# One activation table for the whole projection, and the last row's steps of the projection placed between the first scans

## The chip, the cores and the metric

The kernel runs on one core of a Trainium2 chip. Its engines work side by side, each through its own queue in order: TensorE (PE), VectorE (DVE), ScalarE (ACT), GpSimd (POOL) and SyncE (SP), which issues DMAs. They wait for one another on semaphores. The metric is the device time of one execution in microseconds (us); lower is better.

## The reference, cut to what matters

The program is a residual chain of four layers on a (4, 1024, 128) tensor: a state-space layer (`_L0_attn_a_ref`), a mixture of experts, a long convolution, the mixture again. The change touches the first layer alone.

```python
x_in = jnp.einsum('bsd,de->bse', x, w_in)              # x is layer-normed
proj = jnp.einsum('bsd,dp->bsp', x_in, w_x)
dt_low, Bm, Cm = jnp.split(proj, [DT_RANK, DT_RANK + D_STATE], axis=-1)
dt = jax.nn.softplus(jnp.einsum('bsr,rd->bsd', dt_low, w_dt) + b_dt) * (DT_MAX - DT_MIN) + DT_MIN
A = -jnp.exp(A_log)
...
def step(h, inp):
    dtt, ut, bt, ct = inp
    dA = dtt[:, :, None] * A
    barA = jnp.exp(dA)
    inp_term = jnp.einsum('bdn,bn,bd->bn', dA, bt, ut)
    h = barA * h + inp_term[:, None, :]
    y = jnp.einsum('bdn,bn->bd', h, ct) + Dp * ut
    return (h, y)
...
x = x + _L0_attn_a_ref(_layernorm(x, axis=-1), ...)
```

## The kernel before, in words

The four batch entries are called rows 0 to 3, each of 1024 tokens. `project` prepares them one after the other, `scan` runs the recurrence; both are queued on the same engines without a barrier between them.

Row b goes through `project` in these steps. DVE normalizes it and PE transposes it, ACT copies it (`tokens`), and PE multiplies it by four folded weights, each in two halves of 512 tokens. The results land in PSUM banks 2 to 5, from which ACT takes them (`projections`: Abs L326, then three copies L328 to L332) and DVE takes the positive part of the first (`positive`, L388). The softplus is max(z,0) + ln(1 + exp(-|z|)): ACT makes the exponential over 1024 columns (`exponential`, L338) and the logarithm (`logarithm`, L306), and DVE adds (`softplus`, L395). DVE multiplies by u (`step_times_u`, L402, tile `dtu`), PE multiplies that by A (`step_products`, L491) and DVE multiplies the result into the scan's input term (`input_rows`, L412).

The step sizes are also split into three bf16 parts in one buffer, `part`: ACT casts the first (`first_part`, L311), POOL subtracts (`remainder`, L268), ACT casts the second (`second_part`, L315), DVE makes the third (`third_part`, L407). SP then stores `part` to DRAM (`steps`, L244), waits until it has landed, counts up `parts_free`, and loads it back in another layout (`stack`, three DMAs, L248). There is one `part` buffer for all rows, so `first_part` of row b waits until `parts_free` has counted b stores. After the fourth row SP issues eight DMAs of zeros into `slots` (L238).

`scan` works through 16 groups of eight channels per row. For group u: PE broadcasts the steps from `stack` into two banks (`broadcast`, two matmuls, L571), ACT makes exp(scale x + bias) in place (L633, "the decay"), DVE scans 1024 steps (L668), and the result is multiplied by `c_rows` (L648), on DVE for u = 1, 4, 7, 10 and 13 and otherwise on POOL. The multiplication of DVE for u stands behind scan u+1. PE sums the states later (L582). Three pairs of banks go round, so `broadcast` of u needs the scan of u-3. Row 0 is written out; rows 1 to 3 are a hardware loop, and PE waits for the `stack` of all of them at the end of row 0.

The order of the work is what the code writes down. What is left of the projection's last row when scans begin is held in `late`: a table by engine that says ahead of which u of row 0 a step is queued. Before the change these are, for row 3, `first_part` (ACT, ahead of u=1), `second_part` (ACT, 3), `step_products` (PE, 3), `third_part` (DVE, 3) and `input_rows` (DVE, 4).

Of the kernel before, what the change touches and what calls it, by code (L numbers as in the profile page):

```python
# [24 lines left out]
P = 128  # L25
# [58 lines left out]
class Plan:  # L84
# [11 lines left out]
    def sb(self, name, shape, dt=F32):  # L96
        return self.memory.enter_context(self.nc.sbuf_tensor(name, shape, dt))
# [78 lines left out]
def project(plan, ps, m, t):  # L176
# [33 lines left out]
    steps_out = plan.dma_sem("steps_out")  # L210
    m["stacked"] = stacked = [plan.dma_sem(f"stacked{b}") for b in range(BATCH)]
    zero_made, half_made, rstd_done, rest_done = plan.sems("gpsimd", "zero_made half_made rstd_done rest_done")
    moments_done, xn_ready, z_taken, a_made, sp_done, dtu_done, lo_done, inp_done = plan.sems(
        "vector", "moments_done xn_ready z_taken a_made sp_done dtu_done lo_done inp_done")
    fold_psum, xt_psum, z_psum, u_psum, b_psum, c_psum, q_psum = plan.sems(
        "tensor", "fold_psum xt_psum z_psum u_psum b_psum c_psum q_psum")
    fold_done, xt_ready, abs_done, u_taken, b_taken, c_taken, a_exp, ln_done, hi_done, mid_done = plan.sems(
# [38 lines left out]
    @plan.on("gpsimd")  # L256
    def _(pool):
        pool.memset(m["neg_half"][:, :], -0.5).then_inc(half_made, 1)
        pool.memset(m["ones"][:, :], 1.0)
        pool.memset(zero[:, :], 0.0).then_inc(zero_made, 1)  # L260
        need(pool, half_made, 1)

        def remainder(b):

            need(pool, hi_done, b + 1)
            need(pool, lo_done, b)
            alone(plan, pool, "gpsimd")
            pool.tensor_tensor(rest[:, :], sp_all[:, bass.ds(b * SEQ, SEQ)], part[:, 0:SEQ], ALU.subtract).then_inc(rest_done, 1)  # L268

        def deviation(b):  # L270
            for q in range(2):
                need(pool, moments_done, b * 2 + (q + 1))
                pool.tensor_tensor(rstd[:, q, :], spread[:, q, :], m["neg_half"][:, 0:HT], ALU.pow).then_inc(rstd_done, 1)

        deviation(0)
        deviation(1)
        with pool.Fori(1, BATCH - 1) as b:
            for q in range(2):
                need(pool, moments_done, b * 2 + (q + 3))
                pool.tensor_tensor(rstd[:, q, :], spread[:, q, :], m["neg_half"][:, 0:HT], ALU.pow).then_inc(rstd_done, 1)  # L280
            remainder(b - 1)
        remainder(BATCH - 2)
        remainder(BATCH - 1)

    @plan.on("scalar")
    def _(act):
# [71 lines left out]
        projections(BATCH - 1, 1)  # L358
        first_part(BATCH - 2)
        exponential(BATCH - 1)  # L360
        second_part(BATCH - 2)
        logarithm(BATCH - 1)

        late["scalar"] = {1: lambda: first_part(BATCH - 1), 3: lambda: second_part(BATCH - 1)}

    @plan.on("vector")
    def _(dve):
# [57 lines left out]
        for q in range(2):  # L425
# [10 lines left out]
        dve.tensor_scalar(a_range[:, :].rearrange("p (n j) -> p n j", j=GROUP), rep, DT_MAX - DT_MIN, None,  # L436
                          ALU.mult).then_inc(a_made, 1)
        for b in range(BATCH):
            if b > 0:
                positive(b, 1)  # L440
            if b + 2 < BATCH:
                dve.wait_ge(x_in[b + 2], 16)
                statistics_of(b + 2, 0)
                statistics_of(b + 2, 1)
            if 0 < b < BATCH - 1:
                positive(b + 1, 0)
            if b + 2 < BATCH:
                normalize(b + 2, 0)
                normalize(b + 2, 1)
            if b > 0:  # L450
                third_part(b - 1)
                input_rows(b - 1)
            softplus(b)
            step_times_u(b)
        late["vector"] = {3: lambda: third_part(BATCH - 1), 4: lambda: input_rows(BATCH - 1)}

    @plan.on("tensor")
    def _(pe):
# [46 lines left out]
            step_products(b - 1)  # L505
        for q in range(2):
            products(BATCH - 1, q)
        step_products(BATCH - 2)

        need(pe, c_taken, 2 * BATCH)  # L510
        need(pe, z_taken, 2 * BATCH)
        late["tensor"] = {3: lambda: step_products(BATCH - 1)}

# [22 lines left out]
def scan(plan, ps, m, t):  # L538
# [7 lines left out]
    ident = const[:, C_ID:C_ID + P]  # L546
    h = m["states"]
    y_t = m["scratch"][:, 0:SEQ]
    diag = plan.sb("diag", [P, P])
    warm = plan.sb("warm", [P, 1])  # L550
    dt_psum, summed, y_psum = plan.sems("tensor", "dt_psum summed y_psum")
    decay_ready, y_taken = plan.sems("scalar", "decay_ready y_taken")
    scanned, prod_dve, x_added, row_moments, diag_made = plan.sems("vector", "scanned prod_dve x_added row_moments diag_made")
    prod_pool, row_pow = plan.sems("gpsimd", "prod_pool row_pow")
    n_dve, n_pool = len(ON_DVE), GROUPS - len(ON_DVE)
    group = lambda u: QG * (u % QUARTERS) + u // QUARTERS
# [63 lines left out]
    def _(act):  # L620
# [2 lines left out]
            need(act, summed, 2 * QG * b + (2 * QG - 1 + q))  # L623
            act.copy(y_t[:, q * HALF:(q + 1) * HALF], bank(ps, 6 + q)).then_inc(y_taken, 1)


        act.activation(warm[:, :], m["bias_p"][:, 0:1], ACT.Exp)
        def row(b, behind):
            for u in range(GROUPS):
                if not behind and u in m["late"]["scalar"]:  # L630
# [19 lines left out]

    @plan.on("vector")
    def _(dve):
        dve.wait_ge(m["skip_in"], 16)
        dve.tensor_scalar(diag[:, :], ident, m["skip"][:, 0:1], None, ALU.mult).then_inc(diag_made, 1)

        def add_to_x(b, q):
            need(dve, y_psum, 2 * b + (q + 1))
            rows = x[:, bass.ds(b * BT + q * HT, HT), 0:D]
# [795 lines left out]
```

## Time and profile before

| | |
|---|---|
| three runs | 553.69, 554.33 and 557.41 us, median 554.33 |
| the profiled execution | 554.59 us, of it a span of 552.7 us |
| busy in the span | PE 303.1, DVE 351.2, ACT 225.1, POOL 302.3 us |
| granted PE clock, mean | 0.73 of full speed |

The span runs from the first instruction to the last; what lies around it is 1.9 us. Projection fills the first 72 us, the scans run until 250 us, then come mixture, convolution and mixture. Queues of different engines overlap, so busy times of engines do not add up to the span; the last instruction's chain of waits does.

### The profile page before, as it was taken

Reading aid. Unit: us, or ns where it says so; the run is one execution under the profiler, and the core shown is the slowest. Engines: PE = TensorE matmul, PEld = TensorE weight load, DVE = VectorE, ACT = ScalarE, POOL = GpSimd, SP = SyncE. Lnnn points to the kernel's source line nnn. Section 1 sums busy time; section 2 is a strip of 40 time slices with the busy share of each in tenths; the row PEclk is TensorE's granted clock in tenths of the full one; section 3 lists DMA queues with packets and bytes.
Section 4 is the critical chain, followed back from the end, with each engine's and each line's share of the span. In section 5 each row is a group of like instructions: output and inputs, shape, how many; then the busy total and the mean of one; then the engine's idle time right before and its main releaser. Section 6 shows DMA issues by size and latency. Waiting matters only on the chain.

```text
span 552.7 us, 5200 instructions
## 1 busy us (share of the span) xinstructions
PE 303.1 (55%) x1283; PEld 154.3 (28%) x1283; DVE 351.2 (64%) x793; ACT 225.1 (41%) x335; POOL 302.3 (55%) x217
## 2 busy tenths in 40 slices
PE   4888552655766656656931394007788665129500
PEld 3333110111111110115820152003466564116300
DVE  5495589999999999996540085035459865207600
ACT  2768972545344445411200393009574211029400
POOL 2141145687686686684577157735342765725772
PEclk9988865777777877876555599557888776559955
DMA  7003436500000000006512231060011202123100
GB/s 202 4 1 114 135 95 225 202 1 1 0 0 0 0 0 0 0 0 180 146 55 63 93 109 43 16 159 1 0 39 38 67 27 69 54 98 91 56 18 9
DMA packets 32148, 33.27 MB, mean 60 GB/s; under 512 B 5574, under 2 KB 25053, under 8 KB 32124
## 3 DMA queue, kind: packets, MB, share of 16 engines
q1 hardware_dynamic: 27228, 25.39, 15.5%
q0 software_dynamic: 4096, 6.90, 3.8%
q10 hardware_dynamic: 800, 0.71, 0.5%
q8 instruction: 9, 0.15, 0.1%
q14 instruction: 15, 0.12, 0.1%
HBM read 14.43 MB, written 20.19 MB: 63 GB/s over the span
## 4 chain that ended last, share of the span: by engine, by line
POOL 15%; PE 13%; issue 12%; DVE 5%; ACT 4%; DMA 3%; DVEq 1%; POOLq 0%; ACTq 0%; SPq 0%
POOL slots L899 7%; POOL out L1085 4%; POOL answers L1085 3%; PE ps L1215 2%; PE ps L1283 2%; PE ps L925 2%; PE ps L1005 2%; PE ps L989 1%; ACT scaled L1027 1%; PE ps L996 1%; PE ps L1303 1%; PE ps L810 1%; DMA slots<-x,put 1%; DVE stats L729 1%; DMA x<-answers 1%
## 5 line engine op out<-in xcount | busy, mean ns | idle before, releaser
L648 POOL TENSOR_TENSOR states<-states,c_rows 128x1024 f32<-128x1024 f32 x44 | 119.0, 2707 | 51.1 <-DVE states L668 51.1
L668 DVE TENSOR_TENSOR_SCAN states<-ps,inp 128x1024 f32<-128x1024 f32 x64 | 142.2, 2271 | 2.7 <-ACT ps L633 2.7
L633 ACT ACTIVATE ps<-ps,bias_p,scale_p 128x1024 f32<-128x1024 f32 x64 | 74.5, 1176 | 88.4 <-PE ps L571 88.3
L571 PE MATMUL ps<-stack,sel 96*128 (+1 forms) x128 | 49.4, 486 | 70.0 <-DVE states L668 63.8
L899 POOL DMA_INDIRECT slots<-x,put x64 | 62.6, 978 | 33.0 <-issue 18.3
L582 PE MATMUL ps<-states,red 128*32 128x512 f32 x256 | 45.8, 811 | 1.8 <-POOL states L648 1.8
L1085 POOL DMA_INDIRECT answers<-reply,home x32 | 31.7, 990 | 24.1 <-DVE reply L1072 15.2
L1085 POOL DMA_INDIRECT out<-reply,home x32 | 31.5, 985 | 24.2 <-DVE reply L1072 15.4
L571 PEld LDWEIGHTS ps<-stack,sel 96*128 96x128 bf16 x128 | 8.9, 104 | 123.7 <-DVE states L668 90.9
L1027 ACT ACTIVATE scaled<-rows 128x128 f32<-128x128 f32 x64 | 26.4, 485 | 31.5 <-DMA rows<-slots 31.5
L729 DVE BATCH_NORM_STATS2 stats<-x 128x6 f32<-128x128 f32 x96 | 19.6, 277 | 28.1 <-DMA x<-answers 27.7
L741 POOL TENSOR_TENSOR rstd<-spread,neg_half 128x8 f32<-128x8 f32 x12 | 19.8, 1647 | 22.1 <-DVE neg_mean L735 22.1
L989 PE MATMUL ps<-const,scaled 128*128 128x128 f32 x64 | 12.1, 319 | 35.7 <-ACT scaled L1027 21.0
L1072 DVE SCALAR_TENSOR_TENSOR reply<-ps,rows,kept 128x128 f32<-128x128 f32 x64 | 18.0, 344 | 15.6 <-PE ps L1005 14.6
L268 POOL TENSOR_TENSOR rest<-states,part 128x1024 f32<-128x1024 bf16 (+1 forms) x4 | 8.5, 2127 | 33.9 <-ACT part L311 33.9
L1197 ACT ACTIVATE c_xn<-x,shift,rstd 128x128 f32<-128x128 f32 x32 | 12.7, 483 | 34.8 <-POOL shift L749 34.8
L925 PE MATMUL ps<-const,c_xn 128*128 128x128 f32 x32 | 7.8, 390 | 34.3 <-ACT c_xn L1197 34.2
L1064 DVE TENSOR_SCALAR empty<-rows 128x4 f32<-128x4 f32 x16 | 3.0, 188 | 37.0 <-DMA rows<-slots 35.7
L810 PE MATMUL ps<-w_r,rx_t 128*128 128x8 f32 x128 | 23.8, 323 | 4.3 <-ACT rx_t L933 4.3
L810 PEld LDWEIGHTS ps<-w_r,rx_t 128*128 128x128 f32 x128 | 23.0, 278 | 5.5 <-ACT rx_t L933 5.5
L648 DVE TENSOR_TENSOR states<-states,c_rows 128x1024 f32<-128x1024 f32 x20 | 24.0, 1198 | 0.0
L1241 DVE SCALAR_TENSOR_TENSOR c_s<-c_u,c_w_tap,c_s 128x1024 f32<-128x1024 f32 x16 | 19.8, 1280 | 6.2 <-ACT c_s L1232 5.9
(162 smaller groups left out, 598.5 us busy)
## 6 DMA issues: line engine op xcount, KB each, us to landing
slots<-zero SPq DMA_DIRECT2D x8, 528.0 KB
rows<-slots SPq DMA_DIRECT2D x16, 264.0 KB, 2.9
steps<-part SPq DMA_DIRECT2D x4, 768.0 KB, 3.2
stack<-steps SPq DMA_DIRECT2D x12, 256.0 KB, 4.1
x<-in_x SPq DMA_DIRECT2D x4, 512.0 KB, 6.8
answers<-x SPq DMA_DIRECT2D x4, 512.0 KB, 6.2
x<-answers SPq DMA_DIRECT2D x4, 512.0 KB, 6.1
out<-x SPq DMA_DIRECT2D x4, 512.0 KB, 3.4
```

The source lines that it names most:

```text
L571: last = pe.matmul(bank(ps, 2 * SLOTS[u] + q), sel[0:PARTS * QUARTER, (g % QG) * P:(g % QG + 1) * P], stack[:, g // QG, bass.ds(b * SEQ + ...
L582: last = pe.matmul(ps[c * QUARTER:(c + 1) * QUARTER, (6 + q) * HALF:(7 + q) * HALF], red[:, r * QUARTER:(r + 1) * QUARTER], h[:, (QUARTERS ...
L633: act.activation(slot(u), slot(u), ACT.Exp, scale=m["scale_p"][:, group(u):group(u) + 1], bias=m["bias_p"][:, group(u):group(u) + 1]).then ...
L648: eng.tensor_tensor(h[:, u * SEQ:(u + 1) * SEQ], h[:, u * SEQ:(u + 1) * SEQ], c_rows[:, bass.ds(b * SEQ, SEQ)], ALU.mult).then_inc(done, 1)
L668: dve.tensor_tensor_scan(h[:, u * SEQ:(u + 1) * SEQ], slot(u), inp[:, bass.ds(b * SEQ, SEQ)], 0.0, ALU.mult, ALU.add).then_inc(scanned, 1)
L729: dve.bn_stats(m["stats"][:, first + i, :], m["x"][:, b * BT + first + i, 0:D])
L741: return pool.tensor_tensor(m["rstd"][:, use, tiles], m["spread"][:, use, tiles], m["neg_half"][:, 0:BT], ALU.pow)
L810: last = pe.matmul(self.ps[:, self.LOGITS * HALF + i * EXPERTS:self.LOGITS * HALF + (i + 1) * EXPERTS], self.m["rx_t"][:, n % 2, i * P:(i ...
L899: pool.indirect_dma_start(out=m["slots"][n // BATCH], out_offset=bass.IndirectOffsetOnAxis(m["put"][:, q, i:i + 1], 0), in_=m["x"][:, b * ...
L1027: last = act.activation(m["scaled"][:, e % 2, j * D:(j + 1) * D], rows[:, j, 0:D], ACT.Identity, scale=rows[:, j, FACTOR:FACTOR + 1], bias ...
L1085: pool.indirect_dma_start(out=m["answers"][layer], out_offset=bass.IndirectOffsetOnAxis(m["home"][:, e, j:j + 1], 0), in_=m["reply"][:, e, ...
L1241: last = dve.scalar_tensor_tensor(out=self.s[:, q, s, :], in0=self.u[:, q, s, j:j + SEQ], scalar=self.w_tap[:, s, j:j + 1], in1=self.s[:, ...
```

## The change: what it does

A table load for a set that holds both Exp and Ln is asked for at ACT's start, and no other load stands in the program after that: the six later ones and the one-column Exp L627, which was there to load the table early, are gone. In `late`, three steps of row 3 (`logarithm`, `softplus`, `step_times_u`) and four of row 2 (`second_part`, `step_products`, `input_rows`, `third_part`) are moved from ahead of the scans to places between them, and the steps that were late before stand later. POOL's row 0 is written out so that `remainder` of row 3 can stand ahead of its u=6. The tile `diag`, which PE waits for before its first broadcast, is made two rows earlier in DVE's queue.

```diff
+        act.preload_act_table_set("natural_log_exp_and_others")
...
-        second_part(BATCH - 2)
-        logarithm(BATCH - 1)
-
-        late["scalar"] = {1: lambda: first_part(BATCH - 1), 3: lambda: second_part(BATCH - 1)}
+
+        late["scalar"] = {1: lambda: logarithm(BATCH - 1), 2: lambda: second_part(BATCH - 2), 5: lambda: first_part(BATCH - 1),
+                          10: lambda: second_part(BATCH - 1)}
...
         for b in range(BATCH):
+            if b == BATCH - 1:
+                dve.wait_ge(m["skip_in"], 16)
+                dve.tensor_scalar(m["diag"][:, :], ident, m["skip"][:, 0:1], None, ALU.mult).then_inc(m["diag_made"], 1)
             if b > 0:
                 positive(b, 1)
...
-            if b > 0:
-                third_part(b - 1)
-                input_rows(b - 1)
-            softplus(b)
-            step_times_u(b)
-        late["vector"] = {3: lambda: third_part(BATCH - 1), 4: lambda: input_rows(BATCH - 1)}
+            if b < BATCH - 1:
+                if b > 0:
+                    third_part(b - 1)
+                    input_rows(b - 1)
+                softplus(b)
+                step_times_u(b)
+        late["vector"] = {2: lambda: input_rows(BATCH - 2), 3: lambda: softplus(BATCH - 1), 4: lambda: step_times_u(BATCH - 1),
+                          5: lambda: third_part(BATCH - 2), 8: lambda: input_rows(BATCH - 1), 12: lambda: third_part(BATCH - 1)}
...
-        step_products(BATCH - 2)
...
-        late["tensor"] = {3: lambda: step_products(BATCH - 1)}
+        late["tensor"] = {1: lambda: step_products(BATCH - 2), 6: lambda: step_products(BATCH - 1)}
...
-        remainder(BATCH - 1)
+        late["gpsimd"] = {6: lambda: remainder(BATCH - 1)}
...
-        act.activation(warm[:, :], m["bias_p"][:, 0:1], ACT.Exp)
...
-        dve.wait_ge(m["skip_in"], 16)
-        dve.tensor_scalar(diag[:, :], ident, m["skip"][:, 0:1], None, ALU.mult).then_inc(diag_made, 1)
...
-        with pool.Fori(0, BATCH) as b:
+        def row(b, behind):
             for u in range(GROUPS):
+                if not behind and u in m["late"]["gpsimd"]:
+                    m["late"]["gpsimd"][u]()
                 if u not in ON_DVE:
                     multiply(pool, prod_pool, b, u)
+
+        row(0, False)
+        with pool.Fori(1, BATCH) as b:
+            row(b, True)
```

ACT's queue from the last copy of the projection on. Before (L311 is the cast of `first_part`, L315 that of `second_part`, L338 Exp, L306 Ln, L633 a decay):

```order
L332 COPY c_rows<-ps 128x512
L311 CAST part<-states 128x1024
L338 ACT_TABLE_LOAD
L338 ACTIVATE states<-states 128x1024
L315 CAST part<-rest 128x1024
L306 ACT_TABLE_LOAD
L306 ACTIVATE states<-states 128x1024
L627 ACT_TABLE_LOAD
L627 ACTIVATE warm<-bias_p 128x1
L633 ACTIVATE ps<-ps,bias_p,scale_p 128x1024
L311 CAST part<-states 128x1024
L633 ACTIVATE ps<-ps,bias_p,scale_p 128x1024 x2
```

And with the change (the same steps have the lines L313, L317, L340, L308 and L635):

```order
L334 COPY c_rows<-ps 128x512
L313 CAST part<-states 128x1024
L340 ACTIVATE states<-states 128x1024
L635 ACTIVATE ps<-ps,bias_p,scale_p 128x1024
L308 ACTIVATE states<-states 128x1024
L635 ACTIVATE ps<-ps,bias_p,scale_p 128x1024
L317 CAST part<-rest 128x1024
L635 ACTIVATE ps<-ps,bias_p,scale_p 128x1024 x3
L313 CAST part<-states 128x1024
L635 ACTIVATE ps<-ps,bias_p,scale_p 128x1024 x5
```

The three table loads are gone, the Ln and row 2's second cast stand behind decays 0 and 1, and row 3's first cast stands behind five decays, ahead of that of u=5.

DVE's queue of the same stretch with the change (L403 `dtu`, L442 `diag`, L389 `positive`, L667 a scan, L413 `input_rows`, L650 DVE's product, L396 softplus, L408 `third_part`), each row with the semaphores it waits for:

```order
L403 SCALAR_TENSOR_TENSOR dtu<-states,u 128x1024 [waits u_taken,q_psum]
L442 TENSOR_SCALAR diag<-const,skip 128x128 [waits skip_in]
L389 TENSOR_SCALAR states<-ps,b_dt 128x512 [waits abs_done]
L667 SCALAR_TENSOR_TENSOR states<-ps,inp 128x1024 [waits summed,decay_ready] x2
L413 TENSOR_TENSOR inp<-inp,ps 128x1024 [waits q_psum]
L667 SCALAR_TENSOR_TENSOR states<-ps,inp 128x1024 [waits summed,decay_ready]
L650 TENSOR_TENSOR states<-states,c_rows 128x1024 [waits scanned]
L396 TENSOR_TENSOR states<-states 128x1024 [waits ln_done]
L667 SCALAR_TENSOR_TENSOR states<-ps,inp 128x1024 [waits summed,decay_ready]
L403 SCALAR_TENSOR_TENSOR dtu<-states,u 128x1024 [waits u_taken,q_psum]
L667 SCALAR_TENSOR_TENSOR states<-ps,inp 128x1024 [waits summed,decay_ready]
L408 TENSOR_TENSOR part<-rest,part 128x1024 [waits mid_done]
```

Before, DVE went through `third_part` and `input_rows` of row 2, `softplus` and `step_times_u` of row 3 and `diag` ahead of its first scan. Now scans begin right behind `positive`, and these steps stand between them; the row that follows the last one shown is the scan of u=5.

PE's queue with the change, from the last product of the projection on (L490), with L575 the broadcasts, L497 `step_products` and L583 the first sum:

```order
L490 MATMUL ps<-scratch,w_c 128x512
L575 MATMUL ps<-stack,sel 128x512 x2
L497 MATMUL ps<-dtu,a_range 128x512 x2
L575 MATMUL ps<-stack,sel 128x512 x10
L497 MATMUL ps<-dtu,a_range 128x512 x2
L575 MATMUL ps<-stack,sel 128x512 x12
L583 MATMUL ps<-u,diag 128x512
```

Row 2's `step_products` stood ahead of the first broadcast; now it is behind it and ahead of the broadcast of u=1. That of row 3 moved from ahead of u=3 to ahead of u=6.

## Rows read from the trace of the kernel before

**Rows 1.** Stretch 115 to 160: us; busy PE, PEld, DVE, ACT, POOL; PE clock, DMA, GB/s.

```profile
115.00:160.00 45.00, 29.49 (x122) 6.15 (x118) 45.00 (x26) 21.26 (x20) 31.88 (x12) 0.77 0.00 0
```

**Rows 2.** Timeline, first table load after the start: start us, us, engine line op [idle before].

```profile
23.97 1.28 ACT L306 ACT_TABLE_LOAD   x1
...
25.27 1.06 ACT L306 ACTIVATE states<-states 128x1024 f32<-128x1024 f32 x1
26.23 0.67 ACT L326 ACTIVATE states<-ps,b_dt 128x512 f32<-128x512 f32 x1
...
26.93 0.75 DVE L388 TENSOR_SCALAR states<-ps,b_dt 128x512 f32<-128x512 f32 x1 [6.00 <-ACT states L326]
```

**Rows 3.** Timeline of the projection's loop: PE, ACT, then DVE, each in time order.

```profile
36.31 1.98 PE L491 MATMUL ps<-dtu,a_range 128*128 128x512 f32 x4 [2.06 <-DVE dtu L402]
...
37.18 1.28 ACT L338 ACT_TABLE_LOAD   x1
...
40.98 0.59 ACT L330 COPY inp<-ps 128x512 f32 x1 [0.26 <-PE ps L484]
...
48.01 1.05 ACT L311 CAST part<-states 128x1024 bf16 x1 [0.20 <-SPq L246]
...
43.40 1.23 DVE L407 TENSOR_TENSOR part<-rest,part 128x1024 bf16<-128x1024 f32 x1 [0.45 <-ACT part L315]
44.54 1.21 DVE L412 TENSOR_TENSOR inp<-inp,ps 128x1024 f32<-128x1024 f32 x1
45.85 1.23 DVE L395 TENSOR_TENSOR states<-states 128x1024 f32<-128x1024 f32 x1
```

**Rows 4.** Timeline from the projection's end to the first scan: DVE, ACT, then PE.

```profile
61.21 1.23 DVE L402 SCALAR_TENSOR_TENSOR dtu<-states,u 128x1024 f32<-128x1024 f32 x1 [0.16 <-issue]
62.35 0.74 DVE L388 TENSOR_SCALAR states<-ps,b_dt 128x512 f32<-128x512 f32 x1
66.41 1.23 DVE L407 TENSOR_TENSOR part<-rest,part 128x1024 bf16<-128x1024 f32 x1 [3.31 <-ACT part L315]
...
71.38 0.28 DVE L654 TENSOR_SCALAR diag<-const,skip 128x128 f32<-128x128 f32 x1
74.13 6.65 DVE L668 TENSOR_TENSOR_SCAN states<-ps,inp 128x1024 f32<-128x1024 f32 x3 [2.47 <-ACT ps L633]
...
61.92 1.05 ACT L311 CAST part<-states 128x1024 bf16<-128x1024 f32 x1
...
72.92 1.18 ACT L633 ACTIVATE ps<-ps,bias_p,scale_p 128x1024 f32<-128x1024 f32 x1 [2.62 <-PE ps L571]
74.03 1.03 ACT L311 CAST part<-states 128x1024 bf16<-128x1024 f32 x1
74.96 2.28 ACT L633 ACTIVATE ps<-ps,bias_p,scale_p 128x1024 f32<-128x1024 f32 x2
...
62.49 3.28 PE L491 MATMUL ps<-dtu,a_range 128*128 128x512 f32 x4 [3.36 <-DVE dtu L402]
71.87 2.72 PE L571 MATMUL ps<-stack,sel 96*128 96x512 bf16 x6 [6.10 <-issue]
```

**Rows 5.** Timeline where a DVE product, a POOL product and the late `third_part` meet.

```profile
80.70 1.20 DVE L648 TENSOR_TENSOR states<-states,c_rows 128x1024 f32<-128x1024 f32 x1
80.96 3.13 POOL L648 TENSOR_TENSOR states<-states,c_rows 128x1024 f32<-128x1024 f32 x1 [1.27 <-DVE states L668]
81.81 3.36 DVE L407 TENSOR_TENSOR part<-rest,part 128x1024 bf16<-128x1024 f32 x1
...
85.10 2.27 DVE L668 TENSOR_TENSOR_SCAN states<-ps,inp 128x1024 f32<-128x1024 f32 x1
```

**Rows 6.** `stack` DMAs: row 3's issue, all twelve's landing; then DVE where row 1 begins.

```profile
88.47 1.25 SPq L248 DMA_DIRECT2D stack<-steps  x3
...
DMA to landing us min/median/max: 3.2/4.1/5.2
...
116.95 8.83 DVE L668 TENSOR_TENSOR_SCAN states<-ps,inp 128x1024 f32<-128x1024 f32 x4
```

More of the change, by code:

```diff
@@ L212, in project @@
     zero_made, half_made, rstd_done, rest_done = plan.sems("gpsimd", "zero_made half_made rstd_done rest_done")
-    moments_done, xn_ready, z_taken, a_made, sp_done, dtu_done, lo_done, inp_done = plan.sems(
-        "vector", "moments_done xn_ready z_taken a_made sp_done dtu_done lo_done inp_done")
+    moments_done, xn_ready, z_taken, a_made, sp_done, dtu_done, lo_done, inp_done, m["diag_made"] = plan.sems(
+        "vector", "moments_done xn_ready z_taken a_made sp_done dtu_done lo_done inp_done diag_made")
+    m["diag"] = sb("diag", [P, P])
     fold_psum, xt_psum, z_psum, u_psum, b_psum, c_psum, q_psum = plan.sems(
@@ L548, in scan @@
     y_t = m["scratch"][:, 0:SEQ]
-    diag = plan.sb("diag", [P, P])
-    warm = plan.sb("warm", [P, 1])
+    diag, diag_made = m["diag"], m["diag_made"]
     dt_psum, summed, y_psum = plan.sems("tensor", "dt_psum summed y_psum")
     decay_ready, y_taken = plan.sems("scalar", "decay_ready y_taken")
-    scanned, prod_dve, x_added, row_moments, diag_made = plan.sems("vector", "scanned prod_dve x_added row_moments diag_made")
+    scanned, prod_dve, x_added, row_moments = plan.sems("vector", "scanned prod_dve x_added row_moments")
     prod_pool, row_pow = plan.sems("gpsimd", "prod_pool row_pow")
```

## The prediction, made before the changed kernel had run

> **What bounds the kernel now.** I read the stretches by engine first. While rows 1 to 3 are scanned DVE is busy for all 45 of 45 us [rows 1]: scans run at DVE's speed, so whatever changes the time at which row 1's first scan starts moves the whole rest by as much. That time is the end of the second scan's slot in the last row of [rows 6]: u=15 of row 0 starts at 116.95, and one of the four scans there takes 8.83 / 4 = 2.2 us, so row 1 starts at 119.15. I compute only how this number moves. Nothing behind it is edited.
>
> Then the timeline around the first scan. DVE stands idle twice there, 3.31 us ahead of `third_part` at 66.41 (ACT's second cast is behind a table load and an Exp) and 2.47 us ahead of the first scan [rows 4]. The first broadcast starts at 71.87, right behind `diag` (71.38 + 0.28), which is at the end of DVE's projection queue although it needs nothing of it. These 5.8 us are what the change can fill.
>
> **Part 1, the tables.** A load lasts 1.28 us, and the Ln behind the first one starts 25.27 - 23.97 = 1.30 after it [rows 2]. ACT runs through there, its next Abs at 26.23 is what DVE waited 6.00 us for, and everything behind hangs on that: 1.3 us earlier. The next loads are covered. That at 37.18 is followed by an Exp and the projection's copies, and the copies wait for PE again at 40.98 (0.26) [rows 3], so PE paces that stretch, not ACT. The Ln of row 1 feeds the softplus at 45.85, but DVE comes to that only when `third_part` and `input_rows` are through (44.54 + 1.21 = 45.75) [rows 3]; they are released by a cast that stood behind PE's products. So 0. The same pattern stands once more with row 2. The last three (Exp and Ln of row 3, and that for the decays) stand in front of work that part 2 moves, and are counted there. Part 1: **-1.3 us**.
> By the Trainium skill (ScalarE: Activation LUTs, What ACT_TABLE_LOAD costs) a switch costs a further drain, about 2.66 us in all. The trace does not agree: 1.30 from the load's start to the Ln's, with an Exp just ahead of the load. By the page's figure part 1 would be -2.7.
>
> **Part 2, the start.** `dtu` of row 2 starts at 61.21 [rows 4], now at 59.9. Behind it stand `diag` and `positive`: dtu takes 62.35 - 61.21 = 1.14 of the queue, diag about 0.2, positive 0.74. PE's first broadcast needs positive, diag and the copies that ended earlier; it starts at 59.9 + 1.14 + 0.2 + 0.74 + 0.1 = **62.1** instead of 71.87. Behind a broadcast its decay starts after 1.05 and the scan 1.21 later (71.87, 72.92, 74.13 [rows 4]), so the first scan is at 64.4 instead of 74.13: **-9.8 us**, part 1 included. ACT has its cast at 60.6 (61.92 less 1.3; it waits for `part` there) and the Exp at 61.6, done by 62.7 and in time for the decay at 63.15.
>
> **Part 3, what stands between the scans now.** Beside `third_part` and `input_rows` of row 3, which stood there before, DVE has four more steps: `input_rows` of row 2 at 1.1; `softplus` of row 3; `dtu` at 1.14 + 0.16 for the drain ahead of it [rows 4] = 1.3; `third_part` of row 2 at 1.15. The softplus stands where the late `third_part` stood before, right behind DVE's first product. There POOL, which had waited since 80.96 while the product ran to 81.9, went first, and DVE's instruction took 3.36 instead of 1.23 [rows 3, 5]; the next scan started 85.10 - 81.81 = 3.3 after it. I charge the softplus 3.3. Row 3's `third_part` is now behind the product for u=10 with POOL's for u=11 pending, the same pattern, and keeps its 3.3. Sum: 1.1 + 3.3 + 1.3 + 1.15 = **+6.9** (4.8 if the softplus, two f32 inputs from SBUF, is not held up).
>
> **Part 4, the second scan.** PE goes through `step_products` of row 2 between the first two broadcasts. The four passes took 1.98 us at 36.31 and 3.28 at 62.49, after 3.36 us of idleness [rows 3, 4]; now PE stands idle from 57.8 (62.49 - 3.36 - 1.3) to 62.1, so 3.3. A broadcast pair takes 2.72 / 3 = 0.9. The broadcast of u=1 starts at 62.1 + 0.9 + 3.3 = 66.3, its decay at 67.35, the scan at 68.6; DVE is free at 64.4 + 2.2 = 66.6. Ends: 0.7 at the fast price, 2.0 at the slow one. I take **+2.0**. ACT's Ln fits ahead of that decay.
>
> **Part 5, the sixth scan.** This decides. ACT's queue has `first_part` of row 3 ahead of the decay of u=5. That cast overwrites `part`, so it waits until row 2's store has landed; the store waits for row 2's `third_part`; and this now stands on DVE directly ahead of the scan of u=5, which needs that decay. So the round trip is open. From the start of a `third_part` to the cast released by it: 43.40 to 48.01 = 4.6 [rows 3]. Cast to decay: 74.96 - 74.03 = 0.93; decay to scan 1.21 [rows 4]. Together 6.75, less DVE's own 1.15: **+5.6**. Behind DVE's wait stands everything. Before, row 2's `third_part` ended at 67.64 and row 3's cast started at 74.03 [rows 4]: the store was long done. Lower bound 5.4: all three are measured and in a chain.
>
> **Part 6, the row boundary.** Row 3's `third_part` now stands ahead of u=12. From its end to the `stack` issue 88.47 - (81.81 + 3.36) = 3.3; the last of the three goes 0.85 later and lands after 3.2 to 5.2 [rows 6]; then 0.1 + 1.05 + 1.21 to the scan: 9.7 to 11.7 us, median 10.6. DVE has four scans and one product until then, 4 x 2.2 + 1.1 = 9.9. Before, 13 scans covered this. Ends: 0 and 1.8. The eight transfers of zeros are queued right behind this `stack` and behind no other, so I take the long side, **+1.4**.
>
> **Sum.** -9.8 + 6.9 + 2.0 + 5.6 + 1.4 = +6.1 us. The profiled execution took 554.59 us; 560.7. The median of the runs is 554.33, 0.3 lower, within what this sum can tell. A change under 1% (5.5 us, so 548.8 to 559.9) is what a measurement here can't well tell from none. As a check, DVE's idle time: 5.8 are gone and 1.3 won in front; new are 2.4 ahead of the first scan, 2.0, 5.6, 1.4 and 2.1 inside the softplus, together 13.5; 13.5 - 7.1 = 6.4.
>
> **Rivals.**
> A, as summed. 0.43.
> B, POOL gets in ahead of `dtu` too. The drain puts dtu 0.16 behind the scan's end [rows 4]; POOL's product for u=3 starts 0.18 behind such an end (80.96 against 74.13 + 6.65 = 80.78). If POOL is first, dtu takes 3.36 instead of 1.23: +2.1, **562.8**. For it: a near tie. Against: DVE leads by 0.02, and nothing here shows a SCALAR_TENSOR_TENSOR held up. 0.24.
> The Trainium skill (SBUF — State Buffer, Who interferes with whom) says that a DVE instruction with two SBUF inputs is blocked for all of a POOL instruction that reads SBUF, whoever issues first going first; by that rule B is possible, and [rows 5] agree with it in either order.
> C, the covers hold better: `stack` lands at the short end, and PE has its clock back in part 4. 6.1 - 1.4 - 1.3 = +3.4, **558.0**, within 1%. 0.16. Against it: PE's clock was down at 62.49 after less idleness.
> D, not slower, one mechanism: ACT is what paces the projection's loop, and each load ahead of row 2's dtu counts. The four I set at 0 (two Exp, two Ln) would give 4 x 1.28 = 5.1: +1.0, **555.6**. It decides once the loads hold up PE's products or DVE's softplus by over 1.3 us in all. Against it: the waits of 0.26 and 0.45 behind the loads [rows 3]. 0.09.
> E, the drain of part 1 counts: a switch gives 2.7 instead of 1.3, so +4.7, **559.3**. For it speaks no row. 0.03. That is the page's rule named in part 1.
> That the loads stay is excluded by the queue as shown. Without the round trip of part 5, and with C as well, it would be 554.6 + 3.4 - 5.6 = 552.4; I see no way to this with one `part` buffer. 0.05 for all that I have not seen, most of it on the fast side.
>
> **Numbers.** 560.7. A spreads from 559.4 to 562; of it 0.37 lies above 559.9, and all of B: slower by over 1% 0.61. C, D, E and the rest of A: within 1% 0.35. Faster 0.04. The range takes in B and its spread above and C below, 557.6 to 564.0; D and the unseen are left out.
>
> **What would show it.** First scan near 64.4. The first broadcast at 62.1 with four passes of step_products behind it. The second scan 4.2 behind the first. A wait of DVE for the decay of about 5.6 ahead of u=5, and on ACT a wait for SP ahead of its second cast in row 0. A softplus of 3.3 us, and `dtu` of 1.2 (B: 3.3). A short wait at the first scan of row 1, which starts near 125.3. ACT with one table load. I am wrong if DVE is busy through u=5, or if the first scan comes well before 64.

## The result: slower by 1.3%, near the forecast

| | us |
|---|---|
| before | 553.69 to 557.41, median 554.15 (4 runs) |
| changed | 560.45 to 564.03, median 562.44 (4 runs) |
| changed to before | 1.0129, 95% interval 1.0099 to 1.0159 |
| profiled execution of the changed kernel | 564.03, span 562.1 |

The forecast was 560.7, in a range of 557.6 to 564.0. The time went where it said: the first scan starts earlier, and DVE then waits between the scans. Two of its terms were off. The gain of 1.3 us that it took from the tables (part 1) was gone before the first scan, and the wait at the row boundary (part 6) was a microsecond longer.

DVE's timeline in the changed kernel, from the last `dtu` ahead of the scans to row 1, stands against [rows 4], [rows 5] and [rows 6]. The line numbers have shifted: L403 is `dtu`, L667 a scan, L413 `input_rows`, L650 DVE's product, L396 softplus, L408 `third_part`.

```profile
61.64 1.23 DVE L403 SCALAR_TENSOR_TENSOR dtu<-states,u 128x1024 f32<-128x1024 f32 x1 [0.16 <-issue]
62.79 0.28 DVE L442 TENSOR_SCALAR diag<-const,skip 128x128 f32<-128x128 f32 x1
62.98 0.75 DVE L389 TENSOR_SCALAR states<-ps,b_dt 128x512 f32<-128x512 f32 x1
66.09 2.29 DVE L667 TENSOR_TENSOR_SCAN states<-ps,inp 128x1024 f32<-128x1024 f32 x1 [2.36 <-ACT ps L635]
70.36 2.29 DVE L667 TENSOR_TENSOR_SCAN states<-ps,inp 128x1024 f32<-128x1024 f32 x1 [1.98 <-ACT ps L635]
72.57 1.20 DVE L413 TENSOR_TENSOR inp<-inp,ps 128x1024 f32<-128x1024 f32 x1
73.68 2.28 DVE L667 TENSOR_TENSOR_SCAN states<-ps,inp 128x1024 f32<-128x1024 f32 x1
75.88 1.20 DVE L650 TENSOR_TENSOR states<-states,c_rows 128x1024 f32<-128x1024 f32 x1
77.17 3.19 DVE L396 TENSOR_TENSOR states<-states 128x1024 f32<-128x1024 f32 x1
80.28 2.28 DVE L667 TENSOR_TENSOR_SCAN states<-ps,inp 128x1024 f32<-128x1024 f32 x1
82.72 1.23 DVE L403 SCALAR_TENSOR_TENSOR dtu<-states,u 128x1024 f32<-128x1024 f32 x1 [0.16 <-issue]
83.86 2.28 DVE L667 TENSOR_TENSOR_SCAN states<-ps,inp 128x1024 f32<-128x1024 f32 x1
86.06 1.20 DVE L408 TENSOR_TENSOR part<-rest,part 128x1024 bf16<-128x1024 f32 x1
92.75 2.29 DVE L667 TENSOR_TENSOR_SCAN states<-ps,inp 128x1024 f32<-128x1024 f32 x1 [5.48 <-ACT ps L635]
...
112.56 3.37 DVE L408 TENSOR_TENSOR part<-rest,part 128x1024 bf16<-128x1024 f32 x1
...
123.52 2.28 DVE L667 TENSOR_TENSOR_SCAN states<-ps,inp 128x1024 f32<-128x1024 f32 x1
127.67 2.29 DVE L667 TENSOR_TENSOR_SCAN states<-ps,inp 128x1024 f32<-128x1024 f32 x1 [1.87 <-ACT ps L635]
130.27 4.47 DVE L667 TENSOR_TENSOR_SCAN states<-ps,inp 128x1024 f32<-128x1024 f32 x2 [0.31 <-ACT ps L635]
```

Three bracketed waits are new (1.98, 5.48, and 1.87 with 0.31 at the row's start). Without a wait, the step behind a scan starts 2.2 us after the scan did; from 86.06 to 92.75 DVE did one step of 1.1 us.

What held up the scan of u=5 is told by the other queues: ACT's, then SP's, in the same kernel.

```profile
71.19 3.37 ACT L635 ACTIVATE ps<-ps,bias_p,scale_p 128x1024 f32<-128x1024 f32 x3
90.59 1.04 ACT L313 CAST part<-states 128x1024 bf16<-128x1024 f32 x1 [16.03 <-SPq L247]
91.54 3.36 ACT L635 ACTIVATE ps<-ps,bias_p,scale_p 128x1024 f32<-128x1024 f32 x3
...
87.29 0.34 SPq L245 DMA_DIRECT2D steps<-part  x1
90.56 1.25 SPq L249 DMA_DIRECT2D stack<-steps  x3
```

ACT sat idle for 16.03 us with the decays of u=2 to 4 done, until SP counted up `parts_free`; SP had issued the store at 87.29, when `third_part` (86.06 + 1.20) was through. ACT's idleness itself costs nothing; what costs is the decay of u=5 queued behind this cast, with DVE waiting for it.

### The profile page after: what moved, and what is told of

Same layout as the page of the kernel before. It is cut to its first block, busy times and chain, and to the rows that moved or that the text cites. A ratio compares the mean times of both kernels' runs of the same rounds, so it can differ in the third digit from the quotient of the medians.

```text
span 562.1 us, 5177 instructions
## 1 busy us (share of the span) xinstructions
PE 309.3 (55%) x1283; PEld 156.6 (28%) x1283; DVE 353.5 (63%) x793; ACT 214.4 (38%) x326; POOL 303.1 (54%) x217
## 4 chain that ended last, share of the span: by engine, by line
POOL 16%; issue 12%; PE 11%; DVE 5%; ACT 4%; DMA 3%; DVEq 1%; POOLq 0%; ACTq 0%; SPq 0%
POOL slots L904 7%; POOL out L1090 4%; POOL answers L1090 3%; PE ps L1288 2%; PE ps L1308 2%; PE ps L1001 2%; PE ps L1010 2%; DVE stats L734 1%; PE ps L815 1%; ACT scaled L1032 1%; PE ps L994 1%; PE ps L930 1%; POOL x L1266 1%; POOL c_v L1258 1%; DMA slots<-x,put 1%
## 5 line engine op out<-in xcount | busy, mean ns | idle before, releaser
L650 POOL TENSOR_TENSOR states<-states,c_rows 128x1024 f32<-128x1024 f32 x44 | 120.1, 2730 | 68.2 <-DVE states L667 68.2
L667 DVE TENSOR_TENSOR_SCAN states<-ps,inp 128x1024 f32<-128x1024 f32 x64 | 142.9, 2278 | 12.0 <-ACT ps L635 12.0
L635 ACT ACTIVATE ps<-ps,bias_p,scale_p 128x1024 f32<-128x1024 f32 x64 | 74.3, 1176 | 85.7 <-PE ps L575 85.4
L575 PE MATMUL ps<-stack,sel 96*128 (+1 forms) x128 | 50.7, 500 | 70.6 <-DVE states L667 64.4
L586 PE MATMUL ps<-states,red 128*32 128x512 f32 x256 | 48.0, 847 | 0.9 <-POOL states L650 0.9
L575 PEld LDWEIGHTS ps<-stack,sel 96*128 96x128 bf16 x128 | 9.5, 106 | 124.6 <-DVE states L667 91.6
L650 DVE TENSOR_TENSOR states<-states,c_rows 128x1024 f32<-128x1024 f32 x20 | 24.1, 1204 | 0.0
L1258 POOL TENSOR_TENSOR c_v<-c_s 128x1024 f32<-128x1024 f32 x4 | 9.4, 2354 | 25.4 <-DVE c_s L1246 25.4
```

The lines of the kernel that those rows point to most:

```text
L575: last = pe.matmul(bank(ps, 2 * SLOTS[u] + q), sel[0:PARTS * QUARTER, (g % QG) * P:(g % QG + 1) * P], stack[:, g // QG, bass.ds(b * SEQ + ...
L586: last = pe.matmul(ps[c * QUARTER:(c + 1) * QUARTER, (6 + q) * HALF:(7 + q) * HALF], red[:, r * QUARTER:(r + 1) * QUARTER], h[:, (QUARTERS ...
L635: act.activation(slot(u), slot(u), ACT.Exp, scale=m["scale_p"][:, group(u):group(u) + 1], bias=m["bias_p"][:, group(u):group(u) + 1]).then ...
L650: eng.tensor_tensor(h[:, u * SEQ:(u + 1) * SEQ], h[:, u * SEQ:(u + 1) * SEQ], c_rows[:, bass.ds(b * SEQ, SEQ)], ALU.mult).then_inc(done, 1)
L667: dve.tensor_tensor_scan(h[:, u * SEQ:(u + 1) * SEQ], slot(u), inp[:, bass.ds(b * SEQ, SEQ)], 0.0, ALU.mult, ALU.add).then_inc(scanned, 1)
```

## The experiments

Ratios are to runs of the kernel before on the same chip, with their 95% intervals. Experiments 1, 4, 5 and 9 ran on a chip on which the kernel before took 569.35 us, 2, 6, 7 and 8 on one where it took 554.78, and 3 and 10 to 12 on one where it took 554.60. So ratios, and the times of the scans in the trace, are compared, not the totals; the microseconds in the expectations are meant at the level of 554.

**1. One table alone.** To the kernel before:

```diff
+        act.preload_act_table_set("natural_log_exp_and_others")
...
-        act.activation(warm[:, :], m["bias_p"][:, 0:1], ACT.Exp)
```

> The kernel before with part 1 of the change alone: one table load, no warming Exp. Theory (PE's clock takes the gain back): DVE's positive part of row 1 starts at 25.7 instead of 26.9 and row 0's step_products at 35.05 instead of 36.31, but the four passes take 3.0 instead of 2.0 us because the granted clock is down, dtu of row 2 starts near 61.6 as in the changed kernel (61.2 before), the first scan at 74.1 to 74.6: ratio to before 1.000 to 1.001. Rival (the loss of 1.7 us between 35 and 40 us in the changed kernel is from its other edits or chance): dtu at 59.9, first scan at 72.8, ratio 0.998.

Ratio 0.9985 (0.9945 to 1.0025), which tells nothing by itself. The trace does: DVE's positive part of row 1 at 25.89, `dtu` of row 2 at 61.86, 35.97 us later, against 61.21 - 26.93 = 34.28 before [rows 2, 4]; first scan at 74.78, 0.2 us later than forecast, as is the positive part. The theory held: the gain of part 1 is made and lost again. What follows is PE's timeline in the changed kernel, where the same happens (61.64 - 25.67 = 35.97), and its stretches by engine.

```profile
31.10 0.65 PE L482 MATMUL ps<-const,scratch 128*128 128x128 f32 x4 [0.86 <-DVE scratch L382]
32.34 0.65 PE L482 MATMUL ps<-const,scratch 128*128 128x128 f32 x4 [0.59 <-DVE scratch L382]
35.05 2.97 PE L497 MATMUL ps<-dtu,a_range 128*128 128x512 f32 x4 [2.06 <-DVE dtu L403]
37.81 1.78 PE L490 MATMUL ps<-scratch,w_z 128*128 128x512 f32 x2
...
30.00:36.00 6.00, 2.49 (x11) 1.32 (x11) 5.61 (x14) 2.76 (x6) 1.89 (x2) 0.99 0.01 1
36.00:48.00 12.00, 10.47 (x27) 4.76 (x25) 9.21 (x29) 7.46 (x11) 3.32 (x3) 0.86 0.16 66
```

`step_products` of row 0 starts 1.26 us earlier than at 36.31 [rows 3], so part 1's gain had come as far as this. It then takes 2.97 instead of 1.98, and the next product 1.78 instead of 1.02. The granted clock over 36 to 48 us is 0.86 (column behind the five busy times), where the kernel before has this:

```profile
28.00:30.00 2.00, 2.00 (x4) 0.81 (x4) 1.85 (x12) 1.03 (x2) 0.22 (x1) 0.73 0.00 0
30.00:32.00 2.00, 2.00 (x3) 0.68 (x2) 1.85 (x12) 0.59 (x1) 1.54 (x2) 0.50 0.00 0
...
36.00:48.00 12.00, 9.72 (x28) 4.65 (x28) 10.92 (x33) 11.03 (x16) 4.18 (x3) 1.00 0.16 66
```

Its clock had been down too, but from 28 to 32, under products on which DVE did not wait, and was up again for `step_products`.

**2. One table, and PE given work in its pause.** To the kernel of experiment 1, in the projection's loop only (the products go to a bank that `step_products` overwrites):

```diff
+            need(pe, inp_done, b)
+            if not isinstance(b, int):
+                for twice in range(2):
+                    pe.matmul(bank(ps, 6), ident, const[:, 0:HALF], start=True, stop=True)
             need(pe, dtu_done, b + 1)
-            need(pe, inp_done, b)
...
+        pe.wait_ge(consts_in, 16)
```

> The kernel with one table alone, and two idle-time f32 matmuls (four passes, constants into the bank that step_products overwrites) in each turn of PE's projection loop, ahead of its wait for dtu. Only there: some 1.7 us of PE work in a gap of 2 to 2.6 us. In all five kernels with one table, DVE takes 36.0 us (35.7 once) from row 1's positive part to row 2's dtu, against 34.3 before. Theory (the clock is down because PE had paused between 30.2 and 35 us): it stays up, step_products take 2.0 instead of 3.0 and 3.3, and the stretch is 34.3 or less (33 if the second drop of the clock, at 49, goes as well): first scan 1.7 to 3 us earlier than in the kernel with one table. Rival (the clock falls for another reason, or the added work delays step_products): 36 us or more.

Ratio 0.993 (0.9905 to 0.9955). PE's timeline, with L492 the added products and L495 `step_products`, and the stretch behind:

```profile
33.17 1.88 PE L492 MATMUL ps<-const 128*128 128x512 f32 x4
35.32 1.99 PE L495 MATMUL ps<-dtu,a_range 128*128 128x512 f32 x4 [0.27 <-DVE dtu L403]
...
47.52 1.98 PE L495 MATMUL ps<-dtu,a_range 128*128 128x512 f32 x4 [0.72 <-DVE dtu L403]
...
36.00:48.00 12.00, 11.28 (x33) 5.19 (x32) 10.89 (x32) 8.62 (x14) 3.79 (x3) 1.00 0.16 66
```

The clock stays at full over 36 to 48 and `step_products` takes 1.99 and 1.98. From row 1's positive part (26.02) to row 2's `dtu` (58.45) it is 32.43 us, 3.54 less than with one table alone; first scan at 71.37. So the clock took back the gain of part 1. A second drop, which the kernel before has as well (3.03 for the four passes of `step_products` at 48.59), is gone too.

**3. The clock's part in the changed kernel.** The same added lines in the changed kernel.

> The changed kernel with the idle-time matmuls of the projection loop, and nothing else. Theory (the clock's part of the loss is independent of what stands between the scans): row 1's positive part to row 2's dtu in 32.4 instead of 36.0 us, the waits ahead of the second scan, of u=5 and at row 1 stay (2, 5.5, 2.3); 3.5 us less than changed: ratio to before 1.0129 - 0.0064 = 1.0065. Rival (PE's pauses are only moved, the clock is down at the first scans instead): ratio over 1.010.

Ratio 1.0068 (1.0048 to 1.0088). It is 32.44 us from the positive part to `dtu` (26.08, 58.52) instead of 35.97, and the first scan is at 62.96. The 5.48 ahead of u=5 stays, and so do the waits at row 1 (1.74 and 0.31), so what the clock costs in the projection and what the open round trip costs are two things. The wait ahead of the second scan did not stay as expected: 0.99 instead of 1.98, with `step_products` of row 2 at 3.05 instead of 3.62. That is not known to be the added products' doing. The same wait is 1.98 in the profiled executions of experiments 4 and 8 and 1.04 and 0.82 in those of 5 and 6, where nothing was edited that runs ahead of it but the name of a buffer. A single profiled execution of these kernels is uncertain by about 1 us for that reason.

**4. The cast queued later.**

```diff
-        late["gpsimd"] = {6: lambda: remainder(BATCH - 1)}
+        late["gpsimd"] = {8: lambda: remainder(BATCH - 1)}
...
-        late["scalar"] = {1: lambda: logarithm(BATCH - 1), 2: lambda: second_part(BATCH - 2), 5: lambda: first_part(BATCH - 1),
+        late["scalar"] = {1: lambda: logarithm(BATCH - 1), 2: lambda: second_part(BATCH - 2), 7: lambda: first_part(BATCH - 1),
```

> The changed kernel with row 3's first cast ahead of the decay of u=7 instead of u=5 and POOL's remainder ahead of u=8 instead of 6. Theory (the open round trip costs 5.5): the cast still waits until about 90.6 but DVE scans u=5 and 6 meanwhile; DVE's wait of 5.48 ahead of u=5 goes, at most 0.3 comes back ahead of u=7; 562.4 - 5.3 = 557.1. Rival (the wait only moves, to u=7 or to the row boundary, where the stack then lands later): 560 or more.

Ratio 1.0034 (1.0001 to 1.0068), 0.95% or 5.3 us below the changed kernel's. On DVE:

```profile
84.93 1.20 DVE L408 TENSOR_TENSOR part<-rest,part 128x1024 bf16<-128x1024 f32 x1
86.05 2.28 DVE L667 TENSOR_TENSOR_SCAN states<-ps,inp 128x1024 f32<-128x1024 f32 x1
...
89.36 4.53 DVE L667 TENSOR_TENSOR_SCAN states<-ps,inp 128x1024 f32<-128x1024 f32 x2
...
121.08 2.29 DVE L667 TENSOR_TENSOR_SCAN states<-ps,inp 128x1024 f32<-128x1024 f32 x1 [1.93 <-ACT ps L635]
```

No wait at u=5, under 0.1 us at u=7, and the one at the row boundary as it was.

**5. The buffer doubled instead.** Row 3 gets its own `part`; the order is that of the changed kernel.

```diff
+    last_part = sb("last_part", [P, PARTS * SEQ], BF16)
+    of_row = lambda b: last_part if isinstance(b, int) and b == BATCH - 1 else part
...
-            need(act, parts_free, b)
-            act.copy(part[:, 0:SEQ], sp_all[:, bass.ds(b * SEQ, SEQ)]).then_inc(hi_done, 1)
+            if of_row(b) is part:
+                need(act, parts_free, b)
+            act.copy(of_row(b)[:, 0:SEQ], sp_all[:, bass.ds(b * SEQ, SEQ)]).then_inc(hi_done, 1)
```

> The changed kernel with a second part buffer for row 3, so that its first cast waits for no store; the order is untouched. Theory: DVE's wait ahead of u=5 is 0 instead of 5.48, the cast starts when softplus is through (near 80.5), 562.4 - 5.5 = 556.9; the same as with the cast queued later. Rival (it is not the buffer but ACT or PE that is late at u=5): the wait stays over 2 us and the time over 559.

Ratio 1.0019 (0.9982 to 1.0057); the scan of u=5 starts at 86.78, 1.12 after `third_part` at 85.66. Two edits that have nothing else in common, this one and that of experiment 4, both removed the wait. That shows its cause: the one buffer, and the place of the cast that overwrites it.

**6. The last `third_part` earlier.** To the kernel of experiment 5:

```diff
-                          10: lambda: second_part(BATCH - 1)}
+                          7: lambda: second_part(BATCH - 1)}
...
-        late["gpsimd"] = {6: lambda: remainder(BATCH - 1)}
+        late["gpsimd"] = {5: lambda: remainder(BATCH - 1)}
...
-        8: lambda: input_rows(BATCH - 1), 12: lambda: third_part(BATCH - 1)}
+        8: lambda: input_rows(BATCH - 1), 9: lambda: third_part(BATCH - 1)}
```

> The kernel with two part buffers, with row 3's remainder on POOL ahead of u=5, its second cast ahead of the decay of u=7 and its third_part ahead of u=9 instead of u=12; that one stays right behind a DVE product. Theory (the stack lands too late for row 1): with three more scans of cover the waits of 1.99 and 0.31 at the start of row 1 are 0, against the kernel with two part buffers -2.3 us, ratio about 0.998. Rival (they come from PE's sums and clock at the boundary, not from the DMA): over 1 us of waiting stays.

Ratio 0.9977 (0.9958 to 0.9996). Its interval overlaps that of experiment 5, which ran on another chip; the trace decides. DVE's last two groups of row 0 and the start of row 1:

```profile
98.35 3.36 DVE L411 TENSOR_TENSOR last_part<-rest,last_part 128x1024 bf16<-128x1024 f32 x1
...
109.31 6.64 DVE L670 TENSOR_TENSOR_SCAN states<-ps,inp 128x1024 f32<-128x1024 f32 x3
115.87 1.20 DVE L653 TENSOR_TENSOR states<-states,c_rows 128x1024 f32<-128x1024 f32 x1
116.98 8.85 DVE L670 TENSOR_TENSOR_SCAN states<-ps,inp 128x1024 f32<-128x1024 f32 x4
```

Four scans across the boundary in 8.85 us, no wait. PE's row in the changed kernel had named what it waited for there, the DMA into `stack`:

```profile
125.16 1.03 PE L575 MATMUL ps<-stack,sel 96*128 x2 [1.90 <-DMA stack<-steps]
```

**7. `step_products` later.**

```diff
-        late["tensor"] = {1: lambda: step_products(BATCH - 2), 6: ...
+        late["tensor"] = {3: lambda: step_products(BATCH - 2), 6: ...
...
-        late["vector"] = {2: lambda: input_rows(BATCH - 2), 3: lambda: softplus(BATCH - 1), ...
+        late["vector"] = {3: lambda: (input_rows(BATCH - 2), softplus(BATCH - 1)), ...
```

> The changed kernel with row 2's step_products on PE ahead of u=3 instead of u=1, and input_rows of row 2 beside the softplus ahead of u=3. Theory: DVE's wait of 1.98 ahead of the second scan goes (0 to 0.3 left), and input_rows, which reads PSUM, runs beside POOL's product, so that the softplus behind it waits for POOL 1.1 us less: together 3 us, ratio 1.0075 against 1.0129. Rival (the decays or PE are late at u=3 instead): a wait of 1 us or more there, ratio over 1.010.

Ratio 1.0058 (1.0029 to 1.0086), 3.9 us below the changed kernel's, where 3 were forecast; by the trace it is 3.2 from the first scan to that of u=5. The first three scans are one row, without a wait, and the softplus waits 1.1 us less for POOL:

```profile
65.77 6.67 DVE L667 TENSOR_TENSOR_SCAN states<-ps,inp 128x1024 f32<-128x1024 f32 x3 [2.36 <-ACT ps L635]
...
74.78 2.07 DVE L396 TENSOR_TENSOR states<-states 128x1024 f32<-128x1024 f32 x1
```

**8. The softplus later, a miss.**

```diff
-        3: lambda: softplus(BATCH - 1), 4: lambda: step_times_u(BATCH - 1), 5: lambda: third_part(BATCH - 2), ...
+        4: lambda: softplus(BATCH - 1), 5: lambda: (step_times_u(BATCH - 1), third_part(BATCH - 2)), ...
```

> The changed kernel with row 3's softplus ahead of u=4 instead of u=3, and dtu with third_part ahead of u=5: the softplus no longer stands right behind DVE's product while POOL's is pending. Theory (it waited for POOL): 1.23 instead of 3.19 us, the scan of u=4 2.0 us earlier, everything behind it 1.5 to 2.0 earlier; ratio to before 1.009 to 1.010 against 1.0129. Rival (the softplus is as slow anywhere, or dtu is now the one held up): no gain, ratio 1.013.

Ratio 1.0131 (1.0104 to 1.0157): nothing gained, and the theory fell in this form. DVE, then POOL:

```profile
75.71 2.28 DVE L668 TENSOR_TENSOR_SCAN states<-ps,inp 128x1024 f32<-128x1024 f32 x1
78.47 3.13 DVE L396 TENSOR_TENSOR states<-states 128x1024 f32<-128x1024 f32 x1 [0.47 <-issue]
...
78.17 2.34 POOL L651 TENSOR_TENSOR states<-states,c_rows 128x1024 f32<-128x1024 f32 x1 [0.18 <-DVE states L668]
```

The scan ended at 77.99. POOL's product started 0.18 later and the softplus 0.47 later; the softplus ended at 81.60, 1.09 after POOL. It was POOL that held it up, as the theory says, but POOL was first here too. Why the softplus started only after 0.47 is not shown: it stands behind a drain (an instruction that makes DVE finish its earlier work) and a wait for the logarithm, which had ended at 65.92. `dtu` also stands behind a drain and waits long fulfilled, and starts 0.16 behind the end of a scan. In the eight kernels in which it meets POOL's product there, the changed one and those of experiments 3 to 7, 10 and 11, it is ahead and POOL pays: 3.41 us for its product at 82.74 in the changed kernel, against 2.34 at 68.56.

**9. Diag early, the rest in place.** The kernel of experiment 1 with the two lines that make `diag` ahead of row 3's positive part, as in the change.

> The same, and diag made ahead of row 3's positive part; all other steps stay where they were before. Theory: the first broadcast no longer stands behind diag; the scan then waits only for DVE itself, which has third_part, input_rows, softplus and dtu to do: first scan at 71.7 instead of 74.13, so -2.4 us, 551.8 (549.9 if the clock stays up in the projection). Rival (the waits are elsewhere, on ACT's Ln and casts): first scan at 73.5 or later, 553.5 or more.

Ratio 0.9967 (0.9928 to 1.0006), inconclusive in time; in the trace the first scan follows `dtu` (71.20) without a wait, at 72.34, 2.4 us earlier than in experiment 1, as the theory has it.

**10 to 12. Better places.** `all_apart` is the changed kernel with another table:

```diff
+        late["gpsimd"] = {5: lambda: remainder(BATCH - 1)}
...
+        late["scalar"] = {2: lambda: second_part(BATCH - 2), 3: lambda: logarithm(BATCH - 1), 5: lambda: first_part(BATCH - 1),
+                          7: lambda: second_part(BATCH - 1)}
...
+        late["vector"] = {2: lambda: third_part(BATCH - 2), 3: lambda: (input_rows(BATCH - 2), softplus(BATCH - 1)),
+                          4: lambda: step_times_u(BATCH - 1), 7: lambda: third_part(BATCH - 1), 8: lambda: input_rows(BATCH - 1)}
...
+        late["tensor"] = {3: lambda: step_products(BATCH - 2), 8: lambda: step_products(BATCH - 1)}
```

> The changed kernel with other numbers in the late tables alone: row 2's third_part ahead of u=2, input_rows and row 3's softplus ahead of u=3, dtu 4, row 3's third_part 7, input_rows 8; casts of row 2 and 3 on ACT ahead of 2, 5 and 7, Ln 3; step_products on PE ahead of 3 and 8; remainder on POOL ahead of 5. Theory: no round trip stands open (the first cast of row 3 comes 7 us after row 2's third_part, the stack has 9 scans), so DVE has no wait from the first scan on: first scan 66.1, row 1 from 115.5 instead of 119.15: -3.6 us, ratio 0.9935. Rival (a new wait at u=3 to 5 on PE or ACT takes it back): ratio over 0.998.

Ratio 0.991 (0.9886 to 0.9935), 5.0 us where 3.6 were forecast. By the trace row 1 starts at 112.51 + 2.2 = 114.7, 4.4 us earlier than before. With the added products of experiment 2:

> The same with the idle-time matmuls in the projection loop. Theory: both gains add: first scan 62.6, row 1 from 112, -7.1 us, ratio 0.987. Rival (with the projection faster, ACT's casts and the stores are late between the scans): over 0.991.

Ratio **0.9835** (0.9813 to 0.9857), 545.48 us against 554.60: the best version, ahead of both kernels. And experiment 9 with those products:

> One table, diag early and the idle-time matmuls, the late steps where they stood before the change. Theory: first scan 71.4 - 2.4 = 69.0, row 1 from 114, -5.2 us, ratio 0.9905: what is moved between the scans with its places right is worth only 2 us beyond this. Rival (moving is worth nothing over it): equal to the other within 0.1%.

Ratio 0.9871 (0.9851 to 0.9891), also a larger gain than forecast. DVE in the best version:

```profile
62.23 4.47 DVE L671 TENSOR_TENSOR_SCAN states<-ps,inp 128x1024 f32<-128x1024 f32 x2 [2.36 <-ACT ps L639]
66.62 1.51 DVE L408 TENSOR_TENSOR part<-rest,part 128x1024 bf16<-128x1024 f32 x1
68.05 2.28 DVE L671 TENSOR_TENSOR_SCAN states<-ps,inp 128x1024 f32<-128x1024 f32 x1
...
109.04 8.83 DVE L671 TENSOR_TENSOR_SCAN states<-ps,inp 128x1024 f32<-128x1024 f32 x4
```

From the first scan to row 1 it waits for no other engine's result. Row 1 starts at 109.04 + 2.2 = 111.2 against 119.15 before, 7.9 us; I expected 7.1. The ratio makes it 9.1, with 7.9 at the short end of its interval. The intervals of the last two touch (0.9851 to 0.9857), but all five runs of the best version (544.91 to 546.72) lie below all five of the other (547.09 to 547.96), on the same chip. So what the change is after, steps of the last row between the scans, is worth 0.36% (2.0 us) over early `diag` and the busy PE alone, when its places are right.

## Why the prediction was right, point by point

By the profiled executions, part by part of the sum:

| part | forecast | measured | from |
|---|---|---|---|
| 1 and 2, first scan | -9.8 | -8.0 | 66.09 instead of 74.13 |
| 3, steps between | +6.9 | +6.9 | 1.11 + 3.28 + 1.38 + 1.12 |
| 4, second scan | +2.0 | +2.1 | 70.36 - 66.09 - 2.2 |
| 5, scan of u=5 | +5.6 | +5.6 | 92.75 - 86.06 - 1.12 |
| 6, row boundary | +1.4 | +2.4 | 1.95 at the first scan, 0.40 at the next |
| sum | +6.1 | +9.0 | second scan of row 1, 130.27 instead of 121.35: +8.9 |

- **The account was right, the number in part by luck.** Parts 3, 4 and 5 came out to 0.1 us, and part 5, the one that decides, with its mechanism. But parts 1 and 6 missed, and both the same way, by 1.8 and 1.0. The measured 562.44 lies above what rival A alone was given (559.4 to 562), next to the 562.8 of rival B, which did not happen. It is inside the range because B had widened it. (The prediction calls 119.15 the end of the second scan's slot in the last of [rows 6]; it is the end of the first, and the number is right.)
- **Part 1** is where the sum was off most. The step that failed: I took a gain at 26 us to hold through the loop with PE's durations as they were. The 1.3 was there at 35.05, and then PE's clock cost 1.7 (experiments 1 and 2; 0.99 in `step_products`, 0.76 in the next product). So the one table gave nothing ahead of row 2's `dtu`. The four loads that I set at 0 were covered, as said; rival D fell: with the clock up (experiment 2) the stretch from row 1's positive part to row 2's `dtu` is 1.85 us shorter than before, and 1.74 of it is what the drop at 48.59 cost there (3.03 and 1.71 for a `step_products` and the product behind it, against 1.98 and 1.02).
- **Rival E** rested on the 2.66 us that the Trainium skill gives for a switch (ScalarE: Activation LUTs, What ACT_TABLE_LOAD costs). The trace does not agree: without a load an Exp ended at 23.94 and the Ln started at 24.00, against 25.27 with one [rows 2]. 1.27 us came off, the load as the row had it, and no drain.
- **Part 2**: diag and positive part as forecast; the first scan 4.45 after `dtu` against the 4.5 summed.
- **Part 3**: the softplus was held up. `dtu` was not: it started at 82.72 and POOL's product at 82.74, the 0.02 us that had been read off (rival B fell, and B had been a near tie). The Trainium skill (SBUF — State Buffer, Who interferes with whom) says that whoever issues first keeps the other out for all of its instruction. The trace agrees, with 3.19 for the softplus and, the other way round, 3.41 for POOL's product beside `dtu`.
- **Part 4**: 2.1 in this execution; that `step_products` is the cause is shown by experiment 7. Its size depends on PE's clock in the execution: the same wait was about 1 us in the profiles of experiments 3, 5 and 6.
- **Part 5** decided, as forecast; shown twice (experiments 4 and 5).
- **Part 6** was mis-sized. PE got the `stack` at 125.16, 9.2 us after `third_part` had ended (112.56 + 3.37), and 5.1 after the last of its three DMAs was issued (119.22 + 0.85). I had taken the long side because the zeros are queued behind this `stack`. The traces do not bear that out. From issue to landing (shortest, median, longest of the three), row 2's `stack`, with no zeros behind it, and then row 3's took in the changed kernel:

```profile
DMA to landing us min/median/max: 3.3/4.1/4.6
...
DMA to landing us min/median/max: 3.2/4.1/4.7
```

In the kernel before, the longest, 5.2, belongs to row 2's. What I had too short was what lies behind the landing: about 0.4 us or more to PE's first product (5.1 less at most 4.7) where I had 0.1, and 2.5 from there to the scan (127.67), where I had 2.3. And I had left out that PE, with its clock down, had 1.94 us of sums between the first two broadcasts, which gave the 0.40. Experiment 6 shows that more cover removes both.
- The check by idle time said 6.4 and left out the same two things.
- **Rival C** (the covers hold better) fell: the `stack` came late, and PE's clock was down under the `step_products` at 64.64, which took 3.62 us. The stretch from 64 to 68:

```profile
64.00:68.00 4.00, 4.00 (x6) 1.50 (x5) 1.91 (x1) 2.77 (x3) 1.73 (x1) 0.50 0.72 170
```


The median moved by 8.3, the profiled pair by 9.4; the profiled execution is the slowest of the changed kernel's four. By the end of the scans it was 8.6 (253.44 against 244.86 for the first statistics behind them; 244.86, and not 250, is where the scans end before). The rest of 0.8 arose in the stages behind, which were not edited; its cause is open.

## What to carry to other kernels

A step queued ahead of a critical one brings its own waits into that queue: for each, look up which buffer it overwrites and how long the round trip is that frees it, and put as much work between the two ends as it takes (here 4.5 us from the start of a `third_part` to the cast, and 11.7 from its end to the first scan that needs the reload). A gain in front of a TensorE chain is only had when the pauses of TensorE are looked at again, since a shift of 1.3 us moved a drop of the clock from where it was hidden to where it cost 1.7. Where two engines keep each other out, tenths of a microsecond between the event and the start decide which is first, and another place in the queue need not change that (experiment 8); putting work that the other engine does not hold up in between does help (experiment 7).

## What the runs showed of the hardware that I had not expected

- PE's clock, by rows: 0.99 from 30 to 36 us in the changed kernel, while PE was busy for 2.49 of the 6 us; then 0.50 from 36 to 38, although PE was busy for all of it. In experiment 2, where PE was busy for 4.29 of the same 6 us, it stayed at 1.00. Four f32 passes of 128x512 cost 1.98 us at the higher level (2.4 GHz) and 3.62 at the lower (1.2 GHz; the changed kernel at 64.64).
- Useless products made the kernel faster: 3.8 us of them (1.88 and 1.92), off the chain, brought 3.5 us.
- Behind the end of a scan POOL's product started after 0.18 us, `dtu` after 0.16 and the softplus after 0.47. These decide who is first; what makes the 0.47 is open.
